# A cross-attention and mixture-of-experts block: a new order of TensorE's work in the slots that hold expert quads, an earlier k, q, v chain, and odd maxima in a second PSUM bank

## The chip, the cores and the metric

The kernel runs on one core of a Trainium2 chip. The metric is device time in microseconds of one execution. TensorE is PE in the profile (its weight loads PEld), VectorE is DVE, ScalarE ACT, GpSimd POOL and SyncE SP.

## The reference

For 64 sequences of 128 rows with 128 columns, and 77 context rows for each sequence, in f32:

```
x = x + tanh(g_xattn) * attention(layernorm(x), ctx)     # 16 heads of depth 8, softmax over 77 keys
x = x + tanh(g_ffn)   * moe(layernorm(x))                # 8 experts, the 2 best of each row
moe: logits = x Wr + br; gates = softmax over the 2 best logits
     out = sum over the 2 of gate * (relu(x W1[e] + b1[e]) W2[e] + b2[e]),  W1[e] 128x256, W2[e] 256x128
```

## The kernel before, in words

The 64 sequences are 16 groups of four. All engines walk the same list of **slots** t = 8, 9, ..., 101, each with a `slot(t)` function that issues its share in a fixed order written out by hand; u is t // 4 and r is t % 4. Semaphores alone tie the engines together, and each engine takes its instructions in order.

In slot t three sequences are in work. Of sequence mx = t - 8 PE makes four **max products** (`max_scores`, L500, four heads each), from which DVE takes the negated row maxima (`head_max`, L1062). From the fifth sequence on all four go to one PSUM bank, max_bank, so that each waits for DVE's maximum of the one before. Of sequence sc = t - 13 PE makes four **scores** (L523, two PSUM banks in turn, maxima folded in), ACT their exponentials (`exp_scores`, L772), and PE the four **values** products (L537) into bank_oT. Of sequence ob = t - 14 ACT copies bank_oT (`output_rows`, L766), PE turns it (`turn_o`, L550) and DVE normalises it and adds it to x.

Once per group come the **group steps**, spread over the slots by r. They share one PSUM bank, group_bank: k (`project_k`, L460), the turned layernorm rows (`turn_x1`, L466), q (`project_q`, L471), v (`project_v`, L476), each emptied by ACT, and k and q also by DVE (`k_low`, `q_low`), since both are kept as a high and a low bf16 half. They are written to DRAM and read back in stacked form by SP (`store_k`, `stack_k`, `store_q`, `stack_q`); the max products of a group start when its q_st and k_st have landed. The turned second layernorm (`turn_x2`, L486) and the router (`route`, L561, in a free part of max_bank) follow later. The reciprocal roots for the two layernorms are made on POOL (`rstd1_of`, `rstd2_of`), which also scatters rows to the experts and gathers them back by indirect DMAs, paced by `keep_pace` to the max products.

The rows for the experts are handled in chunks of 12 or 8 sequences. When a chunk is routed, its rows are sorted by expert in DRAM, and PE works it off in **quads** of four tiles of 128 rows, one quad in a slot: slots 43 to 50, 55 to 62, 67 to 73 and 75 lie beside the attention, 78 and 79 to 91 behind it. A quad has two halves: `hidden_part` 0 and 1 (L611 to L613) fill the bank hidden_p, ACT empties it with four relus a half (`relu`, L838), and one slot later `rows_out` 0 and 1 (L625, L627) make y, which ACT copies in one piece (`outputs`, L847). The last eight sequences go through all experts densely, behind the attention.

In a slot PE's order is: turned maxima (r = 0 and 2), scores 0, max 0, `project_k` (r = 0) or `project_q` (r = 2), hidden half 0, scores 1, max 1, `turn_o`, `route` (r = 0), y half 0 of the quad before, values 0, scores 2, max 2, y half 1, `turn_x1` (r = 1) or `project_v` (r = 3), values 1, scores 3, max 3, values 2, hidden half 1, `turn_x2` (r = 3), values 3. ACT's order is: turned maxima, copy of bank_oT, exponential 0, high half of k or q, relus of half 0, exponential 1, copy of y of the quad before, exponential 2, copies for `turn_x1` or `project_v`, exponential 3, relus of half 1, and in r = 3 the copies for the second layernorm.

## Time and profile before

| | us |
|---|---|
| runs (3) | 627.59, 634.58, 635.36; median 634.58 |
| profiled execution | 634.84 (span 633.1) |
| PE busy | 556.7 (88%) |
| PE weight loads busy | 399.3 (63%) |
| DVE busy | 369.5 (58%) |
| ACT busy | 356.5 (56%) |
| POOL busy | 272.7 (43%) |
| mean granted TensorE clock | 0.956 of full speed |

PE is busiest; its busy time counts overlapping, modelled ends, so the start of one product against the start of the next says more than the share. The attention runs in slots 8 to 77, up to about 510 us; the quads and the dense part behind it take the rest.

### The profile page before, as it was taken

Reading aid. Unit: us, or ns where it says so; the run is one execution under the profiler, and the core shown is the slowest. Engines: PE = TensorE matmul, PEld = TensorE weight load, DVE = VectorE, ACT = ScalarE, POOL = GpSimd, SP = SyncE. Lnnn points to the kernel's source line nnn. Section 1 sums busy time; section 2 is a strip of 40 time slices with the busy share of each in tenths; the row PEclk is TensorE's granted clock in tenths of the full one; section 3 lists DMA queues with packets and bytes.
Section 4 is the critical chain, followed back from the end, with each engine's and each line's share of the span. In section 5 each row is a group of like instructions: output and inputs, shape, how many; then the busy total and the mean of one; then the engine's idle time right before and its main releaser. Section 6 shows DMA issues by size and latency. Waiting matters only on the chain.

```text
span 633.1 us, 18491 instructions
## 1 busy us (share of the span) xinstructions
PE 556.7 (88%) x6213; PEld 399.3 (63%) x6213; DVE 369.5 (58%) x1361; ACT 356.5 (56%) x834; POOL 272.7 (43%) x283
## 2 busy tenths in 40 slices
PE   3579988999799889899889989999898879999996
PEld 1335555555455567767566767656676658898875
DVE  4466866878977864444865555785554324324364
ACT  2126756656566666656666566666655446656441
POOL 7430001000376003444464344673545456676771
PEclk9858989979999999999999899999999769999999
DMA  4936635634555657554788654495432526685431
GB/s 132 162 93 158 145 102 141 149 95 140 132 162 151 114 109 129 122 95 151 92 171 123 152 105 124 121 160 100 114 85 81 100 60 163 152 151 160 111 109 53
DMA packets 158121, 78.65 MB, mean 124 GB/s; under 512 B 85088, under 2 KB 153312, under 8 KB 158032
## 3 DMA queue, kind: packets, MB, share of 16 engines
q1 hardware_dynamic: 119760, 45.65, 34.2%
q10 hardware_dynamic: 31104, 17.13, 9.9%
q0 software_dynamic: 7168, 14.69, 9.5%
q8 instruction: 54, 0.88, 0.6%
q14 instruction: 35, 0.29, 0.2%
HBM read 30.72 MB, written 36.75 MB: 107 GB/s over the span
## 4 chain that ended last, share of the span: by engine, by line
PE 61%; DVE 12%; DMA 7%; issue 7%; ACT 6%; SPq 2%; ACTq 2%; POOL 2%; another core or an unknown queue 0%; DVEq 0%
PE y L627 13%; PE bank_oT L537 7%; PE scores L523 7%; DVE neg_max L1062 4%; PE max_scores L500 4%; PE hidden_p L611 4%; DMA q_st<-q_dram 3%; PE hidden_p L612 3%; PE max_scores L561 3%; PE o L550 2%; ACT probs L772 2%; DMA q_dram<-q_hl 2%; PE hidden_p L613 2%; PE bank_oT L668 2%; PE group L471 2%
## 5 line engine op out<-in xcount | busy, mean ns | idle before, releaser
L1062 DVE TENSOR_REDUCE neg_max<-max_scores 128x4 f32<-128x308 f32 x244 | 116.1, 476 | 128.9 <-PE max_scores L500 125.1
L772 ACT ACTIVATE probs<-scores 77x512 f32<-77x512 f32 x256 | 148.8, 596 | 50.3 <-PE scores L523 47.8
L1413 POOL DMA_INDIRECT xs_dram<-rows,at x112 | 109.8, 981 | 83.4 <-PE max_scores L500 51.3
L1428 POOL DMA_INDIRECT back<-ys_dram,at x112 | 107.6, 960 | 63.8 <-PE max_scores L500 26.8
L537 PE MATMUL bank_oT<-probs,v_cols 77*9 77x128 f32 x2048 | 104.2, 279 | 9.2 <-ACT probs L772 8.1
L523 PE MATMUL scores<-q_st,k_st 128*77 128x128 bf16 x1024 | 106.9, 229 | 0.3
L523 PEld LDWEIGHTS scores<-q_st,k_st 128*77 128x77 bf16 x1024 | 73.1, 119 | 47.5 <-issue 40.8
L838 ACT ACTIVATE hidden<-hidden_p,b_cols 128x128 f32<-128x128 f32 x256 | 73.6, 374 | 42.6 <-PE hidden_p L613 35.6
L627 PE MATMUL y<-w_sb,hidden 128*128 x608 | 95.0, 296 | 0.0
L500 PE MATMUL max_scores<-k_st,q_st 128*128 128x308 bf16 x244 | 75.4, 309 | 20.5 <-DVE neg_max L1062 12.3
L627 PEld LDWEIGHTS y<-w_sb,hidden 128*128 128x128 f32 x608 | 83.5, 199 | 2.4
L847 ACT COPY ys<-y 128x512 f32<-128x512 f32 x38 | 22.3, 587 | 75.4 <-PE y L627 75.4
L611 PE MATMUL hidden_p<-xsT,w_sb 128*128 128x128 bf16 x256 | 53.6, 229 | 11.5 <-ACT hidden L838 11.2
L1374 POOL TENSOR_TENSOR rstd<-ve,power 128x4 f32<-128x4 f32 x16 | 17.6, 1102 | 105.2 <-DVE ve L1030 105.1
L537 PEld LDWEIGHTS bank_oT<-probs,v_cols 77*9 77x9 f32 x2048 | 30.5, 88 | 50.8 <-ACT probs L772 21.6
L1368 POOL TENSOR_TENSOR rstd<-ve,power 128x4 f32<-128x4 f32 x16 | 17.1, 1068 | 94.4 <-DVE ve L1003 75.9
L613 PE MATMUL hidden_p<-xsT,w_sb 128*128 128x128 bf16 x256 | 53.1, 224 | 0.0
L612 PE MATMUL hidden_p<-xsT,w_lo 128*128 128x128 bf16 x256 | 52.8, 223 | 0.1
L766 ACT COPY oT<-bank_oT 128x512 f32<-128x512 f32 x64 | 37.6, 587 | 13.3 <-PE bank_oT L537 13.2
L500 PEld LDWEIGHTS max_scores<-k_st,q_st 128*128 128x128 bf16 x244 | 24.2, 99 | 32.9 <-DVE neg_max L1062 23.7
L550 PE MATMUL o<-ident,oT 128*128 128x128 f32 x256 | 40.4, 282 | 3.5 <-ACT oT L766 3.3
L611 PEld LDWEIGHTS hidden_p<-xsT,w_sb 128*128 x256 | 25.3, 99 | 27.8 <-issue 23.4
(160 smaller groups left out, 919.3 us busy)
## 6 DMA issues: line engine op xcount, KB each, us to landing
ys_dram<-ys ACTq DMA_DIRECT2D x38, 256.0 KB
q_st<-q_dram SPq DMA_DIRECT2D x16, 512.0 KB, 4.7
k_st<-k_dram SPq DMA_DIRECT2D x64, 77.0 KB
xs_all<-x SPq DMA_DIRECT2D x16, 256.0 KB, 4.2
q_dram<-q_hl SPq DMA_DIRECT2D x16, 256.0 KB
xs_dram<-zeros_b ACTq DMA_DIRECT2D x16, 256.0 KB, 3.0
out<-xs_all SPq DMA_DIRECT2D x16, 256.0 KB
k_dram<-k_hl SPq DMA_DIRECT2D x48, 77.0 KB
```

Of the source, the lines that this page charges most:

```text
L500: mm(max_to(b, h)[:, 0:PER * KEYS], q_st[g % 3][:, h, seq_cut(b, S)], k_st[g % 3][:, h, b % NB, :, :].rearrange("p j k -> p (j k)"), start ...
L523: last = mm(score_bank[h % 2][0:KEYS, j * S:(j + 1) * S], k_st[g % 3][:, h, b % NB, j, :], q_st[g % 3][:, h, seq_cut(b, S)], start=True, s ...
L537: last = mm(oT_bank[ROWS * j:ROWS * j + VW, h * S:(h + 1) * S], v_cols[g % 3][:, b % NB, h * PER + j, :], probs[h][:, j * S:(j + 1) * S], ...
L611: mm(o, w_hi[:, at_w], tiles[:, 0, cut], start=True, stop=False, skip_group_check=True)
L612: mm(o, w1_lo[:, at_w], tiles[:, 0, cut], start=False, stop=False, skip_group_check=True)
L613: last = mm(o, w_hi[:, at_w], tiles[:, 1, cut], start=False, stop=True, skip_group_check=True)
L627: last = mm(o, hidden[:, (2 * q + t // 2) % 4, t % 2, m, :], w2_sb[:, bass.ds(w + m * 128, 128)], start=False, stop=(m == HC - 1), skip_gr ...
L772: nc.scalar.activation(probs[h][:], score_bank[h % 2][0:KEYS, :], ACT.Exp, scale=SCALE).then_inc(s_exp, 1)
L838: last = nc.scalar.activation(hidden[:, k % 4, i, m, :], of[:, j * 128:(j + 1) * 128], ACT.Relu, bias=b1_cols[:, bass.ds(held[q][2 * half ...
L1062: V.tensor_reduce(neg_max[:, i // 2, :, h, i % 2], max_to(b, h)[:, 0:PER * KEYS].rearrange("p (j k) -> p j k", j=PER), AXIS_X, ALU.max, ne ...
L1413: G.indirect_dma_start(out=xs_dram[c % 2], out_offset=bass.IndirectOffsetOnAxis(ap=at[k][c % 4][:, i:i + 1], axis=0), in_=rows[c % 2][:, i ...
L1428: G.indirect_dma_start(out=back[k][:, b % 16, :], out_offset=None, in_=ys_dram[c % 2][0:TILES[c] * 128, :], in_offset=bass.IndirectOffsetO ...
```

## The change

It has three parts, all in the order of the work; no product, copy or transfer is added or taken away.

1. A slot that holds a hidden half or a y part of a quad, up to slot 78 (`early_scores`), gets its own order on PE (`slot_of_quads`): scores 1 stands right behind max 0, the fourth values product of the sequence before comes behind it (it is left out at the end of the slot before), and hidden half 0 stands behind max 1. ACT takes exponential 0 ahead of the copy of bank_oT and exponential 1 ahead of the relus. DVE takes the third maximum ahead of the logits and of the attention's output.
2. Of a group's chain, `project_k` moves from r = 0 to r = 2 of the group before (two slots earlier), `turn_x1` and `project_q` one slot earlier, `project_v` from r = 3 to r = 1, with the copies on ACT and DVE, the first layernorm's statistics and the stores and stacks on SP. In all slots the turned maxima now stand behind max 0 on PE and behind exponential 0 on ACT, and `turn_x2` with its copies stands ahead of values 1 and of exponential 3.
3. Max products 1 and 3 of a sequence go to the bank hidden_p where the slot has no quad (`lent`); `max_before` names the last maximum that must have left the same bank.

```diff
 def ranks_before(s):
...
+def lent(b, h):
+    return h % 2 == 1 and b >= NB and not quads_at(b + MAX_LAG)
 def max_to(b, h):
-    return (max_bank, score_bank[0], score_bank[1], y_bank)[h] if b < NB else max_bank
+    if b < NB:
+        return (max_bank, score_bank[0], score_bank[1], y_bank)[h]
+    return hidden_bank if lent(b, h) else max_bank
...
+def lent_before(s):
+    return max([HG * b + h + 1 for b in range(clip(s - MAX_LAG, B)) for h in range(HG) if lent(b, h)], default=0)
 def dense_before(s):
...
+def early_scores(t):
+    return bool(quads_at(t) or quads_at(t - 1)) and t <= LAST_ATT
+def values_behind(b, t):
+    return active(b) and not early_scores(t + 1)
 def dense_at(s):
...
-        if r == 0 and later_group(u - 1):
-            store_k(u - 1)
...
+            store_q(u - 1)
+        if r == 2 and later_group(u - 1):
+            stack_q(u - 1)
...
-        if r == 2 and later_group(u - 1):
-            store_q(u - 1)
...
-        if r == 2 and u >= 2 and group_on(u):
-            load_ctx(u)
+        if r == 2 and group_on(u + 1):
+            load_ctx(u + 1)
...
-        if r == 3 and later_group(u - 1):
-            stack_q(u - 1)
+        if r == 3 and later_group(u):
+            store_k(u)
...
+    load_ctx(2)
...
     def project_k(g):
...
-        if g >= 4:
-            pe.wait_ge(s_xT2, clip(g - 3, NG))
-        elif g >= FIRST_GROUPS:
+        if g >= FIRST_GROUPS:
...
     def turn_x1(g):
...
+        if g >= 4:
+            pe.wait_ge(s_xT2, g - 3)
...
     def turn_x2(g):
+        pe.wait_ge(s_klo, clip(g + 5, NG))
...
-        n = HG * b + h + 1 - (HG if b < NB else 1)
-        if n > 0:
-            pe.wait_ge(s_max, n)
-        if h == 2 and b % NB == 0 and g >= 3:
+        if max_before(b, h) > 0:
+            pe.wait_ge(s_max, max_before(b, h))
+        if lent(b, h) and quads_before(b + MAX_LAG):
+            pe.wait_ge(s_relu, 2 * quads_before(b + MAX_LAG))
+        if h == (3 if early_scores(b + MAX_LAG) else 2) and b % NB == 0 and g >= 3:
...
     def route(g, t):
...
-        pe.wait_ge(s_max, clip(HG * (t - MAX_LAG) + 2, HG * B))
+        pe.wait_ge(s_max, clip(HG * (t - MAX_LAG) + (3 if early_scores(t) else 1 if lent(t - MAX_LAG, 1) else 2), HG * B))
...
+        if half == 0 and lent_before(QUAD_AT[q]):
+            pe.wait_ge(s_max, lent_before(QUAD_AT[q]))
...
+    def older_maxima(t):
+        u, r = t // NB, t % NB
+        if r == 0 and group_on(u - 3):
+            turn_max(u - 3, 1)
+        if r == 2 and group_on(u - 2):
+            turn_max(u - 2, 0)
+    def first_group_step(t):
+        u, r = t // NB, t % NB
+        if r == 0 and later_group(u - 1):
+            turn_x1(u - 1)
+        if r == 1 and later_group(u - 1):
+            project_q(u - 1)
+    def middle_group_step(t):
+        u, r = t // NB, t % NB
+        if r == 2 and later_group(u):
+            project_k(u)
+        if r == 3 and group_on(u - 4):
+            turn_x2(u - 4)
+    def last_group_step(t):
+        u, r = t // NB, t % NB
+        if r == 1 and later_group(u - 1):
+            project_v(u - 1)
+        for c in range(NC):
+            if t == RANKED[c]:
+                ranks(c)
+    def slot_of_quads(t):
+        u, r = t // NB, t % NB
+        mx, sc, ob = t - MAX_LAG, t - SCORE_LAG, t - OUT_LAG
+        if active(sc):
+            scores(sc, 0)
+        if active(mx):
+            max_scores(mx, 0)
+        if active(sc):
+            scores(sc, 1)
+        if active(ob):
+            values(ob, 3)
+        older_maxima(t)
+        first_group_step(t)
+        if active(mx):
+            max_scores(mx, 1)
+        for q in quads_at(t):
+            hidden_part(q, 0)
+        if active(sc):
+            scores(sc, 2)
+        if active(mx):
+            max_scores(mx, 2)
+        if active(sc):
+            values(sc, 0)
+        if active(ob):
+            turn_o(ob, t)
+        if r == 0 and group_on(u - 5):
+            route(u - 5, t)
+        for q in quads_at(t - 1):
+            rows_out(q, 0)
+        if active(sc):
+            scores(sc, 3)
+            values(sc, 1)
+        middle_group_step(t)
+        for q in quads_at(t - 1):
+            rows_out(q, 1)
+        if active(mx):
+            max_scores(mx, 3)
+        if active(sc):
+            values(sc, 2)
+        for q in quads_at(t):
+            hidden_part(q, 1)
+        last_group_step(t)
+        if values_behind(sc, t):
+            values(sc, 3)
...
+        if early_scores(t):
+            slot_of_quads(t)
+            return
...
-        if r == 0 and later_group(u - 1):
-            project_k(u - 1)
-        if r == 2 and later_group(u - 1):
-            project_q(u - 1)
+        older_maxima(t)
+        first_group_step(t)
         for n in dense_at(t):
...
-        if r == 1 and later_group(u - 1):
-            turn_x1(u - 1)
-        if r == 3 and later_group(u - 1):
-            project_v(u - 1)
+        middle_group_step(t)
...
-        if r == 3 and group_on(u - 4):
-            turn_x2(u - 4)
-        for c in range(NC):
-            if t == RANKED[c]:
-                ranks(c)
-        if active(sc):
+        last_group_step(t)
+        if values_behind(sc, t):
...
-        if r == 0 and later_group(u - 1):
-            k_high(u - 1)
-        if r == 2 and later_group(u - 1):
-            q_high(u - 1)
...
+        if early_scores(t):
+            if active(sc):
+                exp_scores(sc, 0)
+            for q in quads_at(t - 2):
+                store_y(q)
+            if active(ob):
+                output_rows(ob)
+            if active(sc):
+                exp_scores(sc, 1)
+            older_maxima(t)
+            first_group_step(t)
+            for q in quads_at(t):
+                name_biases(q)
+                relu(q, 0)
...
-        if r == 1 and later_group(u - 1):
-            turned_x1(u - 1)
-        if r == 3 and later_group(u - 1):
-            v_columns(u - 1)
-        if active(sc):
-            exp_scores(sc, 3)
-        for q in quads_at(t):
-            relu(q, 1)
+        if r == 2 and later_group(u):
+            k_high(u)
...
+        if active(sc):
+            exp_scores(sc, 3)
+        for q in quads_at(t):
+            relu(q, 1)
+        if r == 1 and later_group(u - 1):
+            v_columns(u - 1)
...
-        if r == 1 and later_group(u - 1):
-            normed1(u - 1)
...
-        if active(t):
-            stats1_of(t)
+        if active(t + 1):
+            stats1_of(t + 1)
...
-        if r == 3 and group_on(u - 4):
-            normed2(u - 4)
-        if r == 0 and later_group(u - 1):
-            k_low(u - 1)
-        if r == 2 and later_group(u - 1):
+        if r == 1 and later_group(u - 1):
...
+        if early_scores(t) and active(mx):
+            head_max(mx, 2)
...
-        if active(mx):
+        if not early_scores(t) and active(mx):
...
-        if active(t):
-            mean_var1(t)
+        if active(t + 1):
+            mean_var1(t + 1)
...
+        if r == 2 and group_on(u - 4):
+            normed2(u - 4)
+        if r == 3 and later_group(u):
+            normed1(u)
...
-        if r == 3 and later_group(u):
+        if r == 2 and later_group(u):
+            k_low(u)
...
+    stats1_of(2 * NB)
+    mean_var1(2 * NB)
...
     def slot(t):
...
-        if r == 0 and later_group(u - 1):
-            rstd1_of(u - 1)
+        if r == 3 and later_group(u):
+            rstd1_of(u)
...
```

## Rows read from the trace of the kernel before

**Rows 1.** Waits: engine, line waited for, us in total, times, longest us.
```profile
PE hidden_p L611 <- ACT hidden L838: 11.2, 13, 1.5
```

**Rows 2.** Windows of slots 37 to 40 together, and of slot 40.
```profile
core 0: us, PE busy (x) PEld busy (x) DVE busy (x) ACT busy (x) POOL busy (x), PEclk, DMA share, GB/s
183.65:205.47 21.82, 19.95 (x258) 12.47 (x254) 16.93 (x64) 14.40 (x28) 15.58 (x16) 1.00 0.55 151
199.44:205.47 6.03, 5.37 (x67) 3.58 (x66) 4.37 (x16) 3.37 (x8) 3.37 (x3) 1.00 0.21 60
```

**Rows 3.** PE lines in slots 37 to 40: count, busy, mean ns, idle before.
```profile
L500 PE MATMUL max_scores<-k_st,q_st 128*128 128x308 bf16 x16 | 4.8, 298 | 1.2 <-DVE neg_max L1062 1.1
...
L561 PE MATMUL max_scores<-wr_sb,xT 128*128 128x8 f32 x8 | 1.1, 259 | 0.4 <-DVE neg_max L1062 0.4
...
L476 PE MATMUL group<-w_att,ctx_in 128*77 128x128 f32 x8 | 1.0, 272 | 0.0
...
L471 PE MATMUL group<-xT,w_att 128*128 128x512 f32 x2 | 1.0, 592 | 0.0
...
L460 PE MATMUL group<-ctx_in,w_att 128*128 128x308 f32 x2 | 0.7, 439 | 0.0
...
L486 PE MATMUL group<-ident,xn 128*128 128x128 f32 x4 | 0.7, 286 | 0.0
```

**Rows 4.** Timeline of PE in slot 37: start, duration, line, count, idle before.
```profile
184.78 0.30 PE L500 MATMUL max_scores<-k_st,q_st 128*128 128x308 bf16 x1 [0.35 <-DVE neg_max L1062]
184.92 0.60 PE L550 MATMUL o<-ident,oT 128*128 128x128 f32 x4
185.45 0.41 PE L537 MATMUL bank_oT<-probs,v_cols 77*9 77x128 f32 x8
...
188.49 0.41 PE L537 MATMUL bank_oT<-probs,v_cols 77*9 77x128 f32 x8 [0.22 <-ACT probs L772]
```

**Rows 5.** Windows: slots 44 to 47; slots 47, 59, 43 and 51 alone.
```profile
224.21:263.34 39.13, 35.86 (x431) 27.08 (x430) 19.71 (x72) 24.22 (x65) 10.22 (x12) 1.00 0.65 116
253.38:263.34 9.96, 9.21 (x117) 7.22 (x113) 4.54 (x18) 6.46 (x18) 3.92 (x5) 1.00 0.70 139
354.68:365.95 11.27, 10.54 (x118) 8.56 (x114) 5.76 (x22) 6.46 (x18) 3.50 (x4) 0.85 0.59 125
217.21:224.21 7.00, 6.88 (x98) 5.02 (x94) 5.84 (x26) 5.10 (x13) 0.72 (x1) 1.00 0.90 189
292.31:300.60 8.29, 7.82 (x93) 5.81 (x89) 4.54 (x18) 5.45 (x13) 3.49 (x4) 1.00 0.33 108
```

**Rows 6.** Timeline of PE in slot 61.
```profile
376.36 0.41 PE L537 MATMUL bank_oT<-probs,v_cols 77*9 77x128 f32 x8
376.70 0.41 PE L523 MATMUL scores<-q_st,k_st 128*77 128x128 bf16 x4
376.95 0.29 PE L500 MATMUL max_scores<-k_st,q_st 128*128 128x308 bf16 x1
377.97 0.23 PE L611 MATMUL hidden_p<-xsT,w_sb 128*128 128x128 bf16 x1 [0.72 <-ACT hidden L838]
...
382.80 0.60 PE L466 MATMUL group<-ident,xn 128*128 128x128 f32 x4
...
384.14 0.41 PE L537 MATMUL bank_oT<-probs,v_cols 77*9 77x128 f32 x8
```

**Rows 7.** Timeline of ACT in slot 61.
```profile
377.08 0.63 ACT L838 ACTIVATE hidden<-hidden_p,b_cols 128x128 f32<-128x128 f32 x2
...
383.00 0.59 ACT L847 COPY ys<-y 128x512 f32<-128x512 f32 x1 [2.13 <-PE y L627]
383.48 0.59 ACT L772 ACTIVATE probs<-scores 77x512 f32<-77x512 f32 x1
```

**Rows 8.** Windows of slots 20 and 24.
```profile
80.88:89.41 8.53, 6.93 (x67) 4.78 (x66) 4.36 (x14) 3.59 (x8) 0.38 (x1) 0.80 0.22 63
105.20:112.33 7.13, 5.49 (x67) 3.56 (x66) 4.26 (x14) 3.52 (x8) 0.39 (x1) 1.00 0.22 65
```

**Rows 9.** Costliest groups of the page: one rstd on POOL.
```profile
L1368 POOL TENSOR_TENSOR rstd<-ve,power 128x4 f32<-128x4 f32 x16 | 17.1, 1068 | 94.4 <-DVE ve L1003 75.9
```

More of the change, by code:

```diff
@@ L301, in ranks_before, with max_before @@
             return len([c for c in range(NC) if RANKED[c] < s])
+        def lent(b, h):
+            return h % 2 == 1 and b >= NB and not quads_at(b + MAX_LAG)
         def max_to(b, h):
-            return (max_bank, score_bank[0], score_bank[1], y_bank)[h] if b < NB else max_bank
+            if b < NB:
+                return (max_bank, score_bank[0], score_bank[1], y_bank)[h]
+            return hidden_bank if lent(b, h) else max_bank
+        def max_before(b, h):
+            if b < NB:
+                return HG * (b - 1) + h + 1
+            n = HG * b + h - 1
+            while n >= HG * NB and lent(n // HG, n % HG) != lent(b, h):
+                n -= 1
+            if n >= HG * NB:
+                return n + 1
+            return 0 if lent(b, h) else HG * (NB - 1) + 1
+        def lent_before(s):
+            return max([HG * b + h + 1 for b in range(clip(s - MAX_LAG, B)) for h in range(HG) if lent(b, h)], default=0)
         def dense_before(s):
@@ L886, in dense_relu, with older_maxima, first_group_step @@
                                          bias=b1_cols[:, j:j + 1]).then_inc(s_drelu, 1)
+            def older_maxima(t):
+                u, r = t // NB, t % NB
+                if r == 0 and group_on(u - 3):
+                    turned_max(u - 3, 1)
+                if r == 2 and group_on(u - 2):
+                    turned_max(u - 2, 0)
+            def first_group_step(t):
+                u, r = t // NB, t % NB
+                if r == 0 and later_group(u - 1):
+                    turned_x1(u - 1)
+                if r == 1 and later_group(u - 1):
+                    q_high(u - 1)
             def slot(t):
@@ L908, in slot @@
                     b2_part(t - 16)
-                if r == 0 and group_on(u - 3):
-                    turned_max(u - 3, 1)
-                if r == 2 and group_on(u - 2):
-                    turned_max(u - 2, 0)
-                if active(ob):
-                    output_rows(ob)
-                for q in quads_at(t - 2):
-                    store_y(q)
-                for n in dense_at(t):
-                    dense_relu(n)
-                if active(sc):
-                    exp_scores(sc, 0)
-                if r == 0 and later_group(u - 1):
-                    k_high(u - 1)
-                if r == 2 and later_group(u - 1):
-                    q_high(u - 1)
-                for q in quads_at(t):
-                    name_biases(q)
-                    relu(q, 0)
-                if active(sc):
-                    exp_scores(sc, 1)
+                if early_scores(t):
[12 more added lines that the diff above has]
+                        relu(q, 0)
+                else:
+                    if active(ob):
+                        output_rows(ob)
+                    for q in quads_at(t - 2):
+                        store_y(q)
+                    for n in dense_at(t):
+                        dense_relu(n)
+                    if active(sc):
+                        exp_scores(sc, 0)
+                    older_maxima(t)
+                    first_group_step(t)
+                    for q in quads_at(t):
+                        name_biases(q)
+                        relu(q, 0)
+                    if active(sc):
+                        exp_scores(sc, 1)
                 for q in quads_at(t - 1):
```

9 lines of the change are left out of this document (3 added, 6 removed).

## The prediction

> **What bounds the kernel now.** I read four views: the waits, to see whom TensorE waits for; windows of one slot each, for what four slots cost; the timeline of one slot of each kind, for the order; and the lines of one window, for the cost of a group step. A slot is one turn t of the planner, r is t modulo 4, and a window runs from one slot's first scores product to the next one's.
>
> The waits show PE idle 11.2 us before the experts' hidden products, until ScalarE's relu has emptied their bank [rows 1]. Idle time starts after a product's modelled end; from start to start a wait costs 0.1 to 0.2 us more.
>
> Four attention-only slots (37 to 40; r = 1, 2, 3, 0) take 21.82 us with PE busy 19.95 and DVE 16.93 [rows 2]. PE idles 1.1 + 0.4 us there for the maxima, which DVE empties out of one bank [rows 3]. In slot 37 the second maximum waits 0.35 us for DVE, and the last values product 0.22 us for the fourth exponential [rows 4].
>
> Four quad slots (44 to 47) take 39.13 us [rows 5]. Slot 61 [rows 6, 7] shows why, as a ring. The last hidden half is issued by 376.36, where values 3 starts; the next one starts at 377.97, 1.02 us after a maximum that takes 0.14 (184.78 to 184.92 in [rows 4]), since the relus between them end only at 377.71. Later the y products are through at 382.80, ScalarE copies y at 383.00, only then can the third exponential (383.48) run, and values 2 starts at 384.14. So the ring is: hidden half 1, its relus, hidden half 0, all products up to the y products, copy of y, exponential, values 2, hidden half 1.
>
> **The change, part by part.** The sum is made against the profiled execution, 634.84 us (span 633.1), which is 0.3 us above the median of the three runs.
>
> *Odd maxima in the experts' bank*, in 39 sequences whose slot has no quad. Removed: the wait of maxima 1 to 3 on the maximum just before, and route's wait for the second one. I walked the four slots in the new order with these spacings: scores 0.25, maximum 0.14, values 0.34, turning o 0.53, ScalarE's operations 0.48 apart and done after 0.59 [rows 4, 6, 7], group steps at their busy time less some 0.15 us by which the last product's end overlaps the next [rows 3]. r = 1 gets project_q and project_v and loses turn_x1: 5.1. r = 2 loses project_q and gets project_k; but ScalarE now copies the turned maxima behind the first exponential, and turning o stands some 0.7 us for that copy: 5.1. r = 3 loses project_v; its last exponential now stands behind two copies (rows, xT2): 4.5. r = 0 loses project_k and gets turn_x1; there the turned maxima wait some 0.5 us for DVE, which has normed2 and k_low in r = 2 and normed1 in r = 3: 5.8. Sum 20.5, so 1.3 us per four slots. Ends: 0, if every wait only moves to an exponential or to DVE; 1.87, if PE's busy time alone is left. I take 1.3, near the 1.5 that [rows 3] give for the maxima. Slots 13 to 42, 52 to 54 and 64 to 66 are 9 such groups: -11.7. Some six slots with routing work on DVE lose more to the maxima; I give them 0.4 each: -2.5 (bounds 0 and -5).
>
> *k, q, v one to two slots forward.* Moved per group: project_k two slots, turn_x1 and project_q one; normed1 and the rstd on POOL; one statistics pair a slot ahead; three k stores, two q stores and the q stack one slot ahead on SP, the context load four. Slot 20 takes 8.53 us and slot 24 7.13, against 6.03 for slot 40 [rows 2, 8]; the first maximum stands there for q_st. A slot's lead (about 5 us) covers that: -2.5 and -1.1, and a quarter more in slot 28: -3.9. On SP the q stack still waits for the q stores to land, now in r = 2, with the store of the first maxima, a load of x and one of the context behind it. Those are read two or more slots later, so I put that at 0 (bounds -1 and +2: at the start the context load shares the DMA engines with the first q stores). POOL's rstd stands behind the scatters of the slot before, DVE's normed1 behind it and the fourth maximum behind that; a late POOL there costs up to 1.07 us a group, one rstd [rows 9], which I put at 0, since normed1 stands late in its slot. The new waits of turn_x1, turn_x2 and of the borrowed bank are for work a slot old: 0.
>
> *Quad slots.* 'Scores ahead' puts the second scores, the held-back fourth values product and a maximum between hidden half 1 and hidden half 0. Of the 1.61 us between the halves (376.36 to 377.97) it covers 0.25 + 0.14 + 0.25 + 0.34 + 0.14, and 0.1 for the second maximum's own wait, so the wait for the relus falls from 0.88 to 0.4. But the ring is not cut: relu still releases hidden half 0, and the third exponential still stands behind the copy of y on ScalarE. What the change takes out of the ring between hidden half 0 and the y products is a maximum (0.14), what it puts in is values 1 (0.34); what covered the ring's other wait, values 1, scores 3 and maximum 3 (0.72 us of the 1.34 between the end of y and values 2), shrinks to a maximum, so that wait grows from 0.6 to 1.2. Net +0.2 us a slot, 20 slots with both parts: +4. Of the group steps, turn_x1 and project_q fill the 0.4 us that is left, project_k, turn_x2 and route lie in the ring, project_v after it: per four slots 3.3 us outside the cover (route 0.9, project_k and turn_x2 0.55 each, 0.3 and 0.4 left of turn_x1 and project_q, 0.6 of project_v [rows 3]), against 2.9 now (39.1 less four rings of 9.04 by the same spacings): +2 over five groups. Slots with a hidden half alone (43, 55, 67; 7.00 us now [rows 5]) have no y to wait for and send their values on: -1.2 each, -3.6. Slots with y alone (51, 63, 74; 8.29 us) get the late exponential, and in r = 3 two copies ahead of the last one: +1.3, +1.3, +0.5. Together +5.5, with bounds of -18 (the whole relu wait goes, 0.88 in 20 slots) and +12 (the 0.6 us by which the y wait grows is paid in full, 20 times).
>
> Sum: -11.7 - 2.5 - 3.9 + 5.5 = -12.6; 634.8 - 12.6 = **622** for the profiled execution and, 0.3 us being nothing here, for the median. The tail from 526 us on keeps its order.
>
> **Rivals.** *The attention slots become PE's stream*: 1.87 x 9 = 16.8 instead of 14.2, 634.8 - 16.8 - 3.9 + 5.5 = 620. For it: DVE is busy only 16.9 of 21.8 us. Against: the exponential waits of [rows 4] and the copies that move ahead of others. The Trainium skill, Perfetto Trace Analysis, section Optimizing Tensor Performance, has the rule: rotate independent matmul groups through different PSUM banks, so that the emptying of one overlaps the next. By that rule this case holds; the trace of before agrees in that a single bank costs the idle time of [rows 3], and leaves open whether anything else takes its place. Chance 0.12.
>
> *The quad slots do shorten*: if hidden half 0 sets their length and the y copy is early enough, 0.88 x 20 = 18 us go: 634.8 - 18.1 - 18 = 599. Against: [rows 7], where the exponential starts 0.48 us after the y copy, though its scores were long there. Chance 0.16.
>
> *The wait for the maxima turns into waits for exponentials and DVE*, and only the q_st waits are won: 634.8 - 3.9 + 5.5 = 636. Chance 0.16.
>
> *Slower: the clock.* In slot 59 the granted clock is 0.85 in the mean, so part of it ran at 1.2 GHz, though PE was busy for 10.54 of its 11.27 us; the like slot 47 took 9.96 at 1.00 [rows 5]: 1.3 us. The new wait before values 2, 1.2 us, is longer than any in slot 61. With n such slots the time is 622 + 1.3 n, 2% slower from n = 20 of the 24 attention slots with a hidden half; all 24 give 653. Against: slots 44 to 47 held both waits of the ring and ran at 1.00. Chance 0.11.
>
> **How the numbers follow.** The forecast has 0.45, its own range 612 to 632. A measurement of this kernel tells about 2% (12.7 us) from no change, so faster means below 622, slower above 647. Faster: 0.2 of the forecast, 0.09 of the stream, 0.16 of the shorter quads, 0.45. Same: 0.25 + 0.03 + 0.16 = 0.44. Slower 0.11. The range 603 to 640 leaves out the clock case and half of the shorter quads.
>
> **What would show it.** Right: four attention slots at about 20.5 us, no wait for q_st in slots 20 and 24, DVE's wait at max_scores nearly gone from PE's list; four quad slots at 39 to 41 us; PE's wait of values on the exponentials grown to some 20 us, that of hidden on relu cut by half. Wrong: quad slots at 8.3 us or less with the y copy not ahead of the wait; attention groups unchanged, with DVE busy over 18 us of 21; or a granted clock well under 1.00 between 217 and 480 us.

## The result and the profile after

The changed kernel takes **654.3 us** (median of 4 runs, 650.1 to 654.9) against 634.0 for the kernel before in the same session: a ratio of 1.033 with the interval 1.024 to 1.041. The forecast was 622, its range ended at 640. The profiled execution took 654.89 us, its span 653.1, 20 more than before. Executions of one kernel fall into faster and slower ones with the granted clock; the ratios are taken from the faster ones, the medians from all.

By stretches, in us, with the two experiments that matter most and the last one:

| stretch | before | after | old order in quad slots | copy of y later | last version |
|---|---|---|---|---|---|
| start to slot 13 | 41.7 | 44.4 | 43.8 | 44.2 | 40.8 |
| attention-only slots (13-42, 52-54, 64-66) | 210.6 | 209.9 | 200.9 | 202.0 | 191.8 |
| slots with quads (43-51, 55-63, 67-75) | 244.3 | 261.6 | 240.4 | 232.2 | 231.4 |
| from slot 76 on | 136.5 | 137.4 | 133.1 | 134.7 | 132.1 |

So the quad slots cost 17.2 us more (forecast +5.5), and the attention-only ones gave 0.7 (forecast 18.1); differences are taken before rounding.

Windows of the changed kernel: slots 37 to 40 and 44 to 47, then 47, 59, 43 and 51, which answer to [rows 2, 5]; 20 and 24, to [rows 8]; last 32, 36 and 52.

```profile
core 0: us, PE busy (x) PEld busy (x) DVE busy (x) ACT busy (x) POOL busy (x), PEclk, DMA share, GB/s
182.46:204.69 22.23, 20.96 (x259) 12.82 (x255) 16.90 (x63) 14.31 (x28) 14.26 (x15) 0.93 0.55 139
223.48:265.24 41.76, 36.03 (x433) 27.32 (x431) 22.17 (x82) 24.27 (x65) 10.92 (x11) 1.00 0.45 108
255.31:265.24 9.93, 8.72 (x104) 6.50 (x105) 4.73 (x17) 6.17 (x16) 5.26 (x6) 1.00 0.56 111
368.99:378.77 9.78, 8.60 (x104) 6.51 (x105) 5.89 (x21) 6.27 (x16) 5.24 (x6) 1.00 0.65 114
216.05:223.48 7.43, 6.16 (x92) 4.22 (x88) 5.72 (x24) 4.83 (x11) 1.01 (x1) 1.00 0.87 120
295.78:305.81 10.03, 7.34 (x90) 5.00 (x88) 4.73 (x17) 5.14 (x12) 4.64 (x5) 0.95 0.27 78
82.72:88.13 5.41, 5.20 (x73) 3.62 (x69) 4.25 (x17) 3.47 (x7) 0.00 (x0) 1.00 0.14 40
103.45:108.99 5.54, 5.27 (x74) 3.63 (x70) 4.49 (x17) 3.48 (x7) 0.00 (x0) 1.00 0.27 65
146.59:156.70 10.11, 8.69 (x74) 5.93 (x70) 6.74 (x29) 3.59 (x7) 0.00 (x0) 0.56 0.12 34
173.28:182.46 9.18, 8.36 (x74) 5.66 (x70) 5.30 (x20) 3.60 (x7) 7.04 (x8) 0.60 0.30 93
305.81:314.79 8.98, 8.98 (x73) 6.13 (x70) 5.13 (x19) 3.57 (x7) 0.14 (x1) 0.50 0.12 35
```

Four quad slots at full clock went from 39.13 to 41.76 us with PE's busy time the same: the 2.6 us are waits. Slots 20 and 24 lost their q_st wait, as forecast (8.53 and 7.13 before). Slots 32, 36 and 52 ran at or near the lower level of 1.2 GHz.

The waits of the changed kernel (columns as in [rows 1]) show who is waited for now; the second line was 8.1 us before.

```profile
PE hidden_p L639 <- ACT hidden L930: 5.8, 6, 2.0
PE bank_oT L563 <- ACT probs L864: 32.7, 44, 1.2
PE o L537 <- DVE nm_hl L1187: 9.1, 5, 4.7
```

The relu wait was halved and the exponential wait grew to more than the forecast 20 us. The third line, 5.3 us before with 1.7 at the longest, now holds one wait of 4.7 us at the start. PE's timeline in slot 61, as in [rows 6]:

```profile
389.53 0.39 PE L549 MATMUL scores<-q_st,k_st 128*77 128x128 bf16 x4
389.85 0.41 PE L563 MATMUL bank_oT<-probs,v_cols 77*9 77x128 f32 x8
390.18 1.13 PE L495 MATMUL group<-xT,w_att 128*128 128x512 f32 x2
391.15 0.29 PE L526 MATMUL max_scores<-k_st,q_st 128*128 128x308 bf16 x1
391.28 0.22 PE L639 MATMUL hidden_p<-xsT,w_sb 128*128 128x128 bf16 x1
...
395.62 0.66 PE L655 MATMUL y<-w_sb,hidden 128*128 x4
396.12 0.29 PE L526 MATMUL max_scores<-k_st,q_st 128*128 128x308 bf16 x1
397.45 0.41 PE L563 MATMUL bank_oT<-probs,v_cols 77*9 77x128 f32 x8 [1.03 <-ACT probs L864]
```

ACT's timeline in the same slot, as in [rows 7]:

```profile
392.25 1.14 ACT L930 ACTIVATE hidden<-hidden_p,b_cols 128x128 f32<-128x128 f32 x4
396.32 0.58 ACT L939 COPY ys<-y 128x512 f32<-128x512 f32 x1 [2.93 <-PE y L655]
396.80 1.08 ACT L864 ACTIVATE probs<-scores 77x512 f32<-77x512 f32 x2
```

ACT stands idle for 2.93 us ahead of the copy of y, with the third exponential's scores long there; then both run, and PE waits 1.03 us for the exponential. In slot 51 the same wait (1.03 us at 303.78) stands ahead of the half-clock stretch that fills slot 52; in slot 63 it is followed by slot 64 at 1.00 (5.41 us).

### The profile page after: what moved, and what is told of

It reads as the page before. It is cut to its first block, busy times and chain, and to the rows that moved or that the text cites. A ratio compares the mean times of both kernels' runs of the same rounds, so it can differ in the third digit from the quotient of the medians.

```text
span 653.1 us, 18511 instructions
## 1 busy us (share of the span) xinstructions
PE 559.4 (86%) x6213; PEld 402.1 (62%) x6213; DVE 377.9 (58%) x1361; ACT 355.9 (54%) x834; POOL 272.3 (42%) x283
## 4 chain that ended last, share of the span: by engine, by line
PE 67%; DVE 11%; issue 8%; ACT 7%; DMA 3%; SPq 1%; ACTq 1%; POOL 1%; another core or an unknown queue 0%; DVEq 0%
PE y L655 12%; PE bank_oT L563 9%; PE scores L549 8%; PE o L576 5%; ACT probs L864 4%; PE hidden_p L639 3%; PE hidden_p L640 3%; PE max_scores L526 3%; DVE neg_max L1177 3%; PE max_scores L587 2%; PE group L495 2%; PE bank_oT L696 2%; PE hidden_p L641 2%; PE o L696 2%; PE y L653 2%
## 5 line engine op out<-in xcount | busy, mean ns | idle before, releaser
L864 ACT ACTIVATE probs<-scores 77x512 f32<-77x512 f32 x256 | 150.5, 597 | 46.6 <-PE scores L549 45.8
L1177 DVE TENSOR_REDUCE neg_max<-max_scores 128x4 f32<-128x308 f32 x166 | 79.3, 478 | 98.7 <-PE max_scores L526 93.4
L563 PE MATMUL bank_oT<-probs,v_cols 77*9 77x128 f32 x2048 | 107.5, 284 | 33.1 <-ACT probs L864 32.7
L549 PEld LDWEIGHTS scores<-q_st,k_st 128*77 128x77 bf16 x1024 | 77.9, 121 | 42.2 <-issue 29.1
L939 ACT COPY ys<-y 128x512 f32<-128x512 f32 x38 | 22.3, 586 | 96.1 <-PE y L655 96.1
L526 PE MATMUL max_scores<-k_st,q_st 128*128 128x308 bf16 x166 | 51.3, 309 | 9.1 <-DVE neg_max L1177 6.9
L576 PE MATMUL o<-ident,oT 128*128 128x128 f32 x256 | 44.1, 299 | 9.0 <-ACT oT L858 7.1
L1177 DVE TENSOR_REDUCE neg_max<-hidden_p 128x4 f32<-128x308 f32 x78 | 36.9, 473 | 14.9 <-PE hidden_p L526 14.3
L576 PEld LDWEIGHTS o<-ident,oT 128*128 128x128 f32 x256 | 30.8, 151 | 18.9 <-issue 9.3
```

What stands on the lines that cost most here:

```text
L526: mm(max_to(b, h)[:, 0:PER * KEYS], q_st[g % 3][:, h, seq_cut(b, S)], k_st[g % 3][:, h, b % NB, :, :].rearrange("p j k -> p (j k)"), start ...
L549: last = mm(score_bank[h % 2][0:KEYS, j * S:(j + 1) * S], k_st[g % 3][:, h, b % NB, j, :], q_st[g % 3][:, h, seq_cut(b, S)], start=True, s ...
L563: last = mm(oT_bank[ROWS * j:ROWS * j + VW, h * S:(h + 1) * S], v_cols[g % 3][:, b % NB, h * PER + j, :], probs[h][:, j * S:(j + 1) * S], ...
L576: last = nc.tensor.transpose(o_bank[:, h * S:(h + 1) * S], oT[:, h * S:(h + 1) * S], ident[:])
L864: nc.scalar.activation(probs[h][:], score_bank[h % 2][0:KEYS, :], ACT.Exp, scale=SCALE).then_inc(s_exp, 1)
L1177: V.tensor_reduce(neg_max[:, i // 2, :, h, i % 2], max_to(b, h)[:, 0:PER * KEYS].rearrange("p (j k) -> p j k", j=PER), AXIS_X, ALU.max, ne ...
```

## The experiments

Theory A: the quad order loses by the copy of y on ACT. Theory B: the moved chain loses by DVE's place for normed1. All ratios are against the kernel before on the same chip.

**1. Old order in the quad slots**, chain and bank as changed.

```diff
 def early_scores(t):
-    return bool(quads_at(t) or quads_at(t - 1)) and t <= LAST_ATT
+    return False
```

> The changed kernel with the order inside the quad slots put back (scores, values product and copies as before), the k, q, v chain and the borrowed bank kept. Between the profiles of before and after, the quad slots (43 to 51, 55 to 63, 67 to 75) cost 17 us more, the attention-only stretches 2 more. Theory A (the new quad order costs the time, by its ring over the copy of y, and by what slot 51 does to slot 52): quad slots back to some 39 us per four, slot 52 back from 9.0 to about 6, 654 - 17 - 3 = 634 us. Theory B (the moved chain costs it: DVE's normed1 ahead of the fourth maximum, PE idle in slots 32 and 36, then a lower granted clock): those slots stay at 10.1 and 9.2 us, and the quad slots, which hold the same chain, stay some 5 us long: 645 to 650 us. The prediction's own sizes (quad order +5.5) would give 649.

622.9 us, ratio 0.980 (0.974 to 0.985). The new order costs 31 us against it by the medians, 35 by the two traces: 21.2 in the quad slots, 9.0 in attention-only slots whose instructions are the same, with more of the half clock there, 4.3 in the tail and 0.6 at the start. That is Theory A's side of the two. Slots 44 to 50 took 66.8 us, against 72.3 in the change and 68.1 before.

**2. The borrowed bank alone**, on the kernel before (`lent`, `max_to`, `max_before` and their waits, as in the diff above).

> The kernel before with the odd maxima of quad-free slots in the experts' bank and nothing else of the change. The prediction's term for this part: 11.7 + 2.5 us less, 634 - 14 = 620 us, four attention slots at 20.5 instead of 21.8. Rival (the waits for maxima turn into waits for exponentials and DVE): 632 to 636 us. Rival (a slot that runs closer has PE idle in longer single spells, and the granted clock falls more often): above 636 us.

622.8 us, ratio 0.980 (0.974 to 0.985). The sum is as forecast, its place is not: the attention-only slots gave 6.3 us, and slots 37 to 40 took 21.9, as before. Start and tail gave 7.6 us, where the code is nearly the same; the mean granted clock was 0.978 against 0.956.

**3. The copy of y behind the third exponential**, in the slots of the new order (the diff leaves out that condition).

```diff
-for q in quads_at(t - 1):
-    outputs(q)
 if active(sc):
     exp_scores(sc, 2)
+for q in quads_at(t - 1):
+    outputs(q)
```

> The changed kernel with ScalarE's copy of y behind the third exponential in the slots of the new order. Theory A (the ring: y products, copy of y, exponential 2, values 2, hidden half 1; PE idle 1.03 us for it in slots 51 and 61): the exponential runs while PE is still at y, the 1.0 us goes in some 20 slots, and with slot 51's idle spell the low granted clock of slot 52 (9.0 us): 654 - 20 - 3 = 631 us, four quad slots at some 36 to 37 us. Rival (hidden half 1 and its relus, or DVE, set the slot's length anyway): 648 to 654 us.

622.4 us, ratio 0.977 (0.969 to 0.985). The window of its slots 44 to 47, columns as above:

```profile
219.03:254.90 35.87, 34.69 (x434) 26.89 (x431) 22.14 (x82) 23.09 (x64) 10.65 (x11) 1.00 0.58 125
```

And ACT's timeline in its slot 61:

```profile
366.23 0.64 ACT L864 ACTIVATE probs<-scores 77x512 f32<-77x512 f32 x1
369.21 0.59 ACT L939 COPY ys<-y 128x512 f32<-128x512 f32 x1 [2.33 <-PE y L655]
369.69 0.59 ACT L864 ACTIVATE probs<-scores 77x512 f32<-77x512 f32 x1
```

The third exponential now runs 3 us ahead of the copy, and the quad slots fall by 29.3 us, 12 below those of the kernel before. Theory A holds, with its number.

**4. normed1 behind the fourth maximum and its split**, in the change.

```diff
-if r == 3 and later_group(u):
-    normed1(u)
 ...
 if r % 2 == 1 and group_on(u - 2):
     max_halves(u - 2, r // 2)
+if r == 3 and later_group(u):
+    normed1(u)
```

> The changed kernel with DVE's four normed1 behind the fourth maximum and the split of the maxima, at the end of r = 3, instead of ahead of them. Theory B (that place makes the turned maxima late, PE idles 1.4 us in slot 32 and 0.8 in slot 36, and the granted clock falls to 0.56 and 0.60 of full there): slots 32, 36 and 37 back from 10.1, 9.2 and 6.9 us to about 6 each, 654 - 4 - 3 - 1.3 = 645 us, a little less if slot 52 also follows. Rival (the idle spell only moves to turn_x1, which waits for normed1, and the clock falls all the same): 652 to 656 us. At the start, the first scores would come before 44.4 us by Theory B, not by the rival.

653.7 us, ratio 1.028 (1.022 to 1.034): Theory B in this form falls. Slots 32 and 36 took 6.1 and 6.2 us, but slot 40 took 9.4: there PE waited 0.87 us for normed1 in turn_x1 instead, and the mean granted clock was 0.59. At 1.00 the place itself is worth little: with normed1 where the change has it slot 32 took 6.9 us in run 3 and slot 36 6.3 in run 1. Slot 52 took 5.4 and slot 64 9.0.

**5 and 6. The later copy of y in the kernel before**, and with the borrowed bank. The edit is that of run 3.

> The kernel before with ScalarE's copy of y behind the third exponential instead of ahead of it, nothing else. Theory A (that copy holds the exponential and so values 2 in every slot with y, in the old order too, where it shows as some 0.6 us of wait): 24 slots lose 0.6 us, 636.5 - 14 = 622 us, a quad slot of r = 1 at 8.6 instead of 9.2 us. Rival (the copy is in the way only in the new order, whose cover of scores 3 and values 1 is gone; in the old one the relus of the two halves set the slot's length): 634 to 637 us.

> The kernel before with the borrowed bank for odd maxima and with the copy of y behind the third exponential. If the two add up (one acts in slots without quads, the other in slots with y): 622.8 - 14 = 609 us by Theory A, 621 to 623 us if the copy's place is nothing in the old order.

625.6 us, ratio 0.985 (0.972 to 0.998), and 621.3, ratio 0.984 (0.973 to 0.994). The expectations start from 636.5 us for the kernel before, which took 631.3 on this chip. Taken as ratios, run 5 lies between its theories; run 6 gains nothing on the bank alone (0.980) and so misses Theory A, though its quad slots took 234.2 us against 243.1 in run 2. In the old order the copy costs about 0.35 us a full slot (68.1 against 65.7 in slots 44 to 50), not 0.6.

**7. The chain alone**: run 1 with `lent` returning False.

> The changed kernel with the old order inside the quad slots and every maximum back in the one bank: what is left of the change is the k, q, v chain one to two slots forward. The prediction's term for it: the waits for q_st in slots 20, 24 and 28 go, 636.5 - 3.9 = 633 us. Rival (the later start, first scores at 43.8 us with the moved chain against 39.2 with the borrowed bank alone, gives that back): 637 to 640 us. Rival (the chain is what the borrowed bank needs to pay): no difference from before, 636 us, while the bank alone had 623 and bank and chain together 623 too, so this one would need both to be worth less together than apart.

633.4 us, ratio 1.001 (0.996 to 1.006). Slots 20 and 24 fell to 5.9 and 6.0 us, but four steady slots (37 to 40) went from 21.8 to 22.3, and the start is 3.4 us later; the quad slots gave 7.9.

**8. Old order and later copy**, chain and bank as changed.

> The changed kernel with the old order inside the quad slots (as in the first run) and the copy of y behind the third exponential; against the run of the new order with that later copy (622.4 us) it tells whether scores ahead are worth anything once the copy is out of the way. Theory A with a gain of 0.6 us in 24 slots of the old order: 622.9 - 14 = 609 us, the new order then costs 13 us even without the copy's wait. Rival (the copy is no wait in the old order): 621 to 624 us, equal to the new order. Rival (the new order has what the copy took): over 623 us, with quad slots above 8.6 us where the new order has 8.2 to 9.3.

613.1 us, ratio 0.969 (0.961 to 0.978). Slots 44 to 50 took 64.2 us; with the new order (run 3) 63.0. Scores ahead are worth 0.17 us a slot there, and slots 51, 63 and 74 lose 4.1 us to them. Over all quad slots the new order is 2.0 us longer (232.2 against 230.2).

**9 and 10. The new order in full slots only**, with the later copy and with the copy as changed.

```diff
-    return bool(quads_at(t) or quads_at(t - 1)) and t <= LAST_ATT
+    return bool(quads_at(t) and quads_at(t - 1)) and t <= LAST_ATT
```

> The changed kernel with the copy of y behind the third exponential, and the new order only in slots that hold both parts (44 to 50, 56 to 62, 68 to 73); slots with a hidden half alone (43, 55, 67) or y alone (51, 63, 74) have the old order. With the later copy, seven full slots took 63.0 us in the new order and 64.2 in the old one, slots 51, 63 and 74 took 26.7 in the new and 22.6 in the old, and slots 43 and 67 14.7 in the new and 12.2 in the old. Theory A (the new order loses where only one part is there, and gains a little in full slots once the copy is away): quads at 225 us against 230 (old order) and 232 (new order everywhere), 613 - 5 = 608 us. Rival (the gain of full slots is made only by what the slots on both sides pay): 612 to 618 us.

> The changed kernel with the new order only in slots that hold both a hidden part and a y part; the copy of y stands ahead of the third exponential as in the change. It tells how much of the change's loss (31 us over the old order with the same chain and bank, 622.9) lies in the six slots with one part, and in the low granted clock behind slots 51 and 63, and how much in the 20 full slots. Theory A (the ring over the copy of y costs in every full slot): full slots as in the change, 72 us for seven, 654 - 4 (y alone) - 3.5 (hidden alone) - 3.5 to 7 (slot 52 or 64 without the low clock) = 640 us. Rival (the six slots and the clock are nearly all of it): 625 to 630 us.

Run 9: 614.0 us, ratio 0.969 (0.962 to 0.977); the quad slots fell to 228.4 us, but slot 56 took 12.2 at a low clock, and the time is in the rival's range. Run 10: median 639.9, from 632.0 us at a mean granted clock of 0.973 to 646.0 at 0.947, too wide to tell its two cases apart by the time. Its trace (633.9 us) tells more: slots 44 to 50 took 72.4 us, as in the change, which is Theory A's side, and the six slots with one part took 11.9 us less than there.

**11 and 12. The b2 split on ACT** at the end of its slot (run 8's kernel), then split and gap exponential in mid-slot (run 9's kernel). The diff is that of the second.

```diff
-if t in (16, 17, 18):
-    b2_part(t - 16)
 ...
     exp_scores(sc, 1)
+if t in (16, 17, 18):
+    b2_part(t - 16)
+for c in range(NC):
+    if t == ROUTED[c] + 2:
+        gap_exponent(c)
 ...
-for c in range(NC):
-    if t == ROUTED[c] + 1:
-        gap_exponent(c)
```

> The changed kernel with the old order in the quad slots, the copy of y behind the third exponential (613.1 us as run before), and ScalarE's three parts of the b2 split (slots 16 to 18; one took 1.04 us) at the end of their slots instead of the start. With the moved chain slot 18 takes 7.9 us, 4.7 before: there the copy of the outputs waits for the split, turning o for the copy with PE idle 1.56 us, and the granted clock falls to 0.79 in the mean. If that idle spell is the cause: slot 18 at 5.3 us and full clock in it, 613 - 2.6 = 610.5 us. Rival (the first part of a b2 split in slot 16 or 17, or the turned maxima, cause it): slot 18 stays at 7.9, 613 us.

> The run with the new order in full slots alone and the later copy of y (614.0 us), with two small ScalarE instructions moved: the three parts of the b2 split (slots 16 to 18) and the exponential of the gap between the two best experts (one per routing, from slot 30) stand behind the second score exponential of their slot, no longer ahead of the copy of the values' output. As they stood, the split (1.04 us) and the wait for DVE's gap held that copy up in slots 18 and 30, turning o stood behind it with PE idle 1.57 and 1.53 us, the granted clock fell, and the slots took 7.9 and 8.2 us against 5.24 of slots 22 and 26. If those idle spells are the cause: slots 18 and 30 at 5.2 to 5.5 us at full clock, 42, 54 and 66 at 5.2 to 5.5 instead of 6.5, 6.4 and 5.7, together -2.5 - 2.7 - 2.2 = 606.5 us. Rival (the low clock comes in some slot or other however PE is fed there): slots 18 and 30 shorter by the idle time alone, a like stretch elsewhere, 611 to 614 us.

Run 11: 614.1 us, ratio 0.968 (0.958 to 0.979), slot 18 still 7.9 us: the end of slot 17 is the same place in ACT's queue as the start of slot 18. Run 12: 606.4 us, ratio 0.958 (0.952 to 0.964), as the first case had it, with slots 18 and 30 at full clock and slots 32 and 40 near half. Its slots 18, 30, 32 and 40:

```profile
71.32:76.56 5.24, 4.65 (x63) 2.48 (x59) 3.83 (x14) 4.54 (x9) 0.30 (x1) 1.00 0.63 186
133.85:139.31 5.46, 5.13 (x76) 2.94 (x73) 5.08 (x23) 3.69 (x9) 1.01 (x1) 1.00 0.66 207
143.93:153.94 10.01, 8.59 (x74) 5.88 (x70) 6.75 (x29) 3.60 (x7) 0.00 (x0) 0.61 0.16 45
192.68:202.81 10.13, 8.68 (x73) 5.93 (x69) 6.91 (x27) 3.60 (x7) 4.00 (x5) 0.56 0.17 49
```

**13. The same two instructions in mid-slot, in the change itself.**

> The changed kernel with only those two ScalarE instructions moved to the middle of their slots; order of the quad slots, copy of y, chain and bank as in the change. If ScalarE's queue accounts for the part of the attention-only slots that the forecast promised and the change did not give: slots 18 and 30 at 5.2 to 5.5 us, slots 13 to 42 at 164 to 166 us instead of 171.7, 654 - 6 = 648 us. If slots 32 and 36 (DVE's part, another idle spell of 0.8 to 1.4 us) keep their low clock, 13 to 42 comes to some 166; if the low clock moves on to slots that had full clock, 168 to 172 and 650 to 654 us.

649.4 us, ratio 1.029 (1.020 to 1.037): slots 18 and 30 at 5.2 and 5.5 us, slots 13 to 42 at 165.8. That is the first case's figure, but not by its cause alone: of the 5.9 us slots 18 and 30 gave 4.0, and slots 36 and 37, whose instructions are the same, 4.3 at a granted clock of 1.00 (0.60 and 0.79 in the change); others lost 2.4. Slot 32 stayed at 10.1.

**14 and 15. POOL's rstd a slot earlier**, in run 12's kernel and in the change itself. In run 12 this chain stands ahead of slot 40's half clock. POOL's timeline there:

```profile
190.69 0.96 POOL L1531 DMA_INDIRECT xs_dram<-rows,at  x1 [0.30 <-issue]
191.68 1.04 POOL L1486 TENSOR_TENSOR rstd<-ve,power 128x4 f32<-128x4 f32 x1
```

DVE's, behind it:

```profile
192.75 1.28 DVE L1125 TENSOR_SCALAR xn<-xs_all,mv,rstd 128x128 f32<-128x128 f32 x4 [1.28 <-POOL rstd L1486]
193.78 0.47 DVE L1177 TENSOR_REDUCE neg_max<-hidden_p 128x4 f32<-128x308 f32 x1
...
194.44 0.18 DVE L1187 TENSOR_TENSOR nm_hl<-neg_max 128x32 bf16<-128x32 f32 x1
```

And PE's, behind that, with the turned maxima:

```profile
194.67 0.31 PE L537 MATMUL o<-ident_b,nm_hl 128*64 128x128 bf16 x1 [1.45 <-DVE nm_hl L1187]
```

The edit, in which `mean_var1` moves as `stats1_of` does, with one more sequence made at the start:

```diff
-if active(t + 1):
-    stats1_of(t + 1)
+if active(t + 2):
+    stats1_of(t + 2)
 ...
 if r == 2 and later_group(u):
     k_low(u)
-    var_eps1(u)
+if r == 1 and later_group(u):
+    var_eps1(u)
 ...
-if r == 3 and later_group(u):
+if r == 2 and later_group(u):
     rstd1_of(u)
```

> The best run so far (606.4 us: chain, borrowed bank, new order in full slots, later copy of y, two ScalarE instructions in mid-slot) with POOL's rstd of the next group's first norm one slot earlier (r = 2), its statistics and DVE's sum with epsilon one slot earlier too. In slot 39 rstd stood behind four scatters of POOL until 192.72, DVE's normed1 behind it, the fourth maximum and its split behind that, the turned maxima at 194.67 with PE idle 1.45 us; slots 32 and 40 then took 10.0 and 10.1 us at half the clock. If that queue is the cause (the step that the prediction put at 0): normed1 no longer waits, slots 32, 36 and 40 at 5.5 to 6.3 us, 606.4 - 4 - 4.2 = 598 us. Rival (DVE is late in r = 3 by its own work, or turn_x1's wait for normed1 takes its place): slots 32 and 40 still 9 to 10 us or another attention slot instead, 604 to 608 us.

> The changed kernel with only that: rstd of the first norm, its statistics and DVE's sum with epsilon one slot earlier. If POOL's queue behind the scatters is what made slots 32 and 36 slow in the change (10.1 and 9.2 us): both at 5.5 to 6.3 us, slot 37 at 5.5, 654 - 4 - 3.2 - 1.4 = 646 us, and in the quad slots of r = 3 and r = 0 nothing lost. Rival: 652 to 655 us, slots 32 or 36 (or 40 in their place) at 9 us or more.

Run 14: **597.7 us**, ratio 0.947 (0.942 to 0.952), faster than both kernels. Run 15: 642.3, ratio 1.016 (1.008 to 1.025), slots 32 and 36 at 6.8 and 6.3 us, first scores at 41.3 instead of 44.4. Run 14's slots 32, 36 and 40, and slots 13 to 42 together:

```profile
139.68:146.50 6.82, 5.26 (x74) 3.63 (x70) 5.91 (x25) 3.60 (x7) 0.00 (x0) 1.00 0.20 57
162.27:168.57 6.30, 5.26 (x73) 3.63 (x70) 5.20 (x20) 3.60 (x7) 4.78 (x6) 1.00 0.40 120
183.89:189.46 5.57, 5.27 (x74) 3.63 (x70) 4.65 (x18) 3.49 (x7) 2.88 (x3) 1.00 0.28 84
40.84:200.53 159.69, 147.04 (x1915) 89.73 (x1913) 134.04 (x507) 109.21 (x213) 43.00 (x41) 1.00 0.61 149
```

The edit took PE's idle spell away in slot 40 alone. In slots 32 and 36 the turned maxima still wait for DVE, first in the change, then in run 14:

```profile
148.56 0.31 PE L537 MATMUL o<-ident_b,nm_hl 128*64 128x128 bf16 x1 [1.43 <-DVE nm_hl L1187]
174.65 0.24 PE L537 MATMUL o<-ident_b,nm_hl 128*64 128x128 bf16 x1 [0.82 <-DVE nm_hl L1187]
141.57 0.24 PE L537 MATMUL o<-ident_b,nm_hl 128*64 128x128 bf16 x1 [1.34 <-DVE nm_hl L1187]
163.64 0.24 PE L537 MATMUL o<-ident_b,nm_hl 128*64 128x128 bf16 x1 [0.82 <-DVE nm_hl L1187]
```

Those two slots are shorter because the granted clock stayed at 1.00, so neither run shows that POOL's queue made them slow. From run 12 to run 14 the traces gained 3.4 us at the start, 4.6 in slots 37 to 40 and 4.4 in slots 32 and 33, the last by the clock; the quad slots lost 7.0, nearly all in slots 56 and 72 at a low clock.

At the start DVE's normed1 and two operations of POOL that split b2 stood side by side in the change; in run 14 (last line) the split comes some 10 us later:

```profile
36.74 1.88 POOL L1553 TENSOR_TENSOR back<-back 96x1024 f32<-96x1024 f32 x1
38.70 1.89 POOL L1555 TENSOR_TENSOR back<-back 32x1024 f32<-32x1024 f32 x1
37.02 4.16 DVE L1125 TENSOR_SCALAR xn<-xs_all,mv,rstd 128x128 f32<-128x128 f32 x4
36.58 1.08 DVE L1125 TENSOR_SCALAR xn<-xs_all,mv,rstd 128x128 f32<-128x128 f32 x4
```

## Why the prediction was wrong, by its steps

The profiled execution missed the forecast by 32.7 us: 17.4 in the attention-only slots, 11.7 in the quad slots, 2.6 at the start and 0.9 from slot 76 on. Two steps failed: the price of the new order in the quad slots, and the granted clock in the attention-only slots, which the sum left out.

*What bounds the kernel.* The ring was right: hidden half 1, relus, hidden half 0, y, copy of y, exponential, values 2. Run 3 cuts it at the copy and the quad slots shorten by 29.3 us.

*"Net +0.2 us a slot"* is the step that failed in the quad slots, and its bound of +12 with it. It counted the work that enters and leaves the ring (+0.34 and -0.14), let PE's wait for the exponential grow by 0.6 us without a price, and took the relu wait of slot 61 for that of every slot. PE's waits in slots 44 to 50, the first two lines before, the third in run 1, the last in the change:

```profile
PE hidden_p L611 <- ACT hidden L838: 2.2, 3, 0.8
PE bank_oT L537 <- ACT probs L772: 1.4, 4, 0.4
PE bank_oT L563 <- ACT probs L864: 1.4, 4, 0.4
PE bank_oT L563 <- ACT probs L864: 7.2, 7, 1.0
```

Run 1, with chain and bank and the old order, has no wait for the relus in these slots, so scores ahead had none left to shorten, and the wait for the exponential, 0.83 us longer a slot, was paid in full: with chain and bank equal the order cost 0.79 us a full slot (72.3 against 66.8 in seven), 14.6 us in all 20. The price of the copy alone, with and without it ahead of the exponential, is 1.33 us in the new order (72.3 against 63.0) and 0.37 in the old one (66.8 against 64.2): nearly 1.0 us more a slot, of which the rest of the order returns 0.17. The old order had the room for it: values 1, scores 3 and the maximum behind y.

*Slots with one part.* "-1.2 each" for 43, 55 and 67 did not come: +0.4, +1.7, +1.1. The last two had mean granted clocks of 0.81 and 0.80; at 1.00, in run 3, these slots took 7.3 us each, +0.2 and -0.1. Hidden half 0 now stands behind the second maximum, and that one waited 1.25 us for DVE at 218.39 in slot 43. For 51, 63 and 74 the forecast was +3.1 and the trace says +4.1.

*Odd maxima, -11.7 and -2.5.* In the slots that the walk described it held: slots 25 to 28 took 20.8 us and, in run 14, 37 to 40 took 20.9, against 20.5 forecast and 22.1 and 21.8 before. It takes bank and chain together: slots 25 to 28 took 21.5 us with the bank alone and 22.2 with the chain alone. With the bank alone slots 37 to 39 gained 0.5 us and slot 40 lost as much, since PE waited 1.21 us for q_st there, a wait that the moved chain takes away.

The attention-only slots gave 0.7 us all the same. Most of what is missing is clock, which the sum put at nothing there: slots 18, 32, 33, 36, 37, 52 and 53 took 56.5 us in the change, at mean granted clocks of 0.50 to 0.89, and with the same instructions 41.4 us at 1.00 (18, 32 and 33 in run 3, 36 and 37 in run 13, 52 and 53 in run 4). Without these 15.1 us the term would be about -16, by estimate. The falls stand beside idle spells of PE behind queues that the walk left out or priced low. ACT's made 1.56 and 1.52 us, where the b2 split and the gap exponential stand ahead of a copy (slots 18 and 30; gone in runs 12 and 13). DVE's made 1.43 and 0.82 us, where normed1 stands ahead of the fourth maximum (slots 32 and 36; 0.62 and 0.75 in run 4); the walk had some 0.5. POOL's made 1.45 us in slot 40 of run 12, the step "which I put at 0, since normed1 stands late"; run 14 took it away, and in the profile of the change slot 40 had no such wait. The Trainium skill, PSUM — Partial Sum Buffer, section Engine vs sequencer instructions, says that the queues of ScalarE, VectorE and GpSimdE are strict FIFO; the rows of run 12 agree, with rstd starting at 191.68, right behind a scatter that began at 190.69.

In run 14 the attention-only slots take 191.8 us, 18.8 less than before, near the 18.1 of the forecast, but partly by luck. Slots 13, 14 and 29 had mean granted clocks of 0.50, 0.74 and 0.57 before and 0.91, 1.00 and 1.00 in run 14, and took 4.8 us less there, which the forecast had not counted.

*Chain, -3.9.* The q_st waits went (slots 20 and 24 now 5.4 and 5.5 us), but the chain alone gave nothing (run 7). The start, put at 0 with bounds -1 and +2, cost 2.6, and not by the context load, for which PE waited 7.4 us in all (7.1 before): DVE's normed1 took 4.16 us beside POOL's split of b2, and the turned maxima waited 4.7 us behind it. In runs 14 and 15 rstd comes earlier, the split later, normed1 took 1.08 and 1.09 us, and the first scores came 3.5 and 3.1 us earlier than in the change.

*The rivals.* Slower came with 0.11, by the clock in quad slots. The 20 full ones ran at 1.00 with that wait in each; the low clock stood in attention slots and in slots 55 and 67. For the ring at full clock, which cost 14.6 us against run 1, I had no case. "The quad slots do shorten" was argued against from the right row [rows 7]: with the copy moved they do, by 12 us where I gave 18.

*Left open.* Which slot gets the low clock changes between runs with the same instructions: slot 32 took 10.1 us in the change and 6.9 in run 3, with PE idle 1.43 and 1.41 us ahead, and 6.3 in run 1, with 0.82; slot 64 took 9.0 us in run 4 and slot 52 in the change; in run 14 slots 56 and 72 took 12.2 and 12.4. What decides it is not settled. The order alone, on the old chain and the single bank, was not tried.

## What to carry to other kernels

Ahead of a reorder, list for every engine in the ring what stands in its queue between two members of the ring, and ask what covered it: a copy that costs 0.4 us under cover costs 1.3 without. Where a step is moved a slot forward, move everything that it waits for on the other queues as well, down to a 1 us operation on POOL, and look at what it will then run beside: normed1 took 4.16 us instead of 1.08. And the place that matters in a queue is the one relative to the next waiting instruction: the end of one slot and the start of the next are the same.

## What the hardware showed

PE idle spells of 0.8 to 1.6 us within a busy stretch stood beside a fall of the granted clock in some executions and not in others. A spell of 1.43 us in slot 32 of the change came with a mean clock of 0.56 and 10.1 us; spells of 1.41 and 1.34 us there, in runs 3 and 14, with 1.00 and 6.9 and 6.8 us. A spell of 0.82 us in slot 36 came with 0.60 and 9.2 us in the change, and with 1.00 and 6.3 us in runs 1 and 14. So the spell itself cost about its length, and the fall some 3 us more in its slot. The 1.0 to 1.2 us before values 2 in each of the 20 full quad slots of the change left the clock there at 1.00.

Four operations of DVE (normed1) took 4.16 us while POOL split b2, and 1.08 us without it. The same kernel differed by 14 us between executions with mean granted clocks of 0.973 and 0.944 (run 10).
